# Balancing's product by columns walked row by row, and a new table of turns

## The reference

```
xn = layernorm(x);  s = attention(xn);  g = silu(ffn(xn));  x = x + s * g
```

```
u = -logsumexp(Z + v, over j);  v = -logsumexp(Z + u, over i)     # 50 times
H = exp(Z + u + v);   mixed_i = sum_j H[i, j] * stream_j
```

## Time and profile before

| | |
|---|---|
| median of three runs | 1274.34 us (1271.59 to 1277.91) |
| the profiled execution | 1270.83 us |
| its span, first to last instruction | 1268.8 us |
| TensorE busy (matmul) | 1050.2 us |
| VectorE busy | 834.3 us |
| ScalarE / GpSimd busy | 565.0 / 328.4 us |
| mean granted TensorE clock | 0.908 |

### The profile page before, as it was taken

How to read it: one execution, slowest core, us unless ns; L and a number is a source line. 1 busy time by engine, 2 the same in 40 slices (tenths; PEclk the granted TensorE clock), 3 DMA queues, 4 the chain that set the end, 5 groups by cost and what they waited for, 6 DMA issues and landing times.

```text
span 1268.8 us, 19873 instructions
## 1 busy us (share of the span) xinstructions
PE 1050.2 (83%) x7480; PEld 444.8 (35%) x7480; DVE 834.3 (66%) x1475; ACT 565.0 (45%) x797; POOL 328.4 (26%) x516
## 2 busy tenths in 40 slices
PE   2889999897898997865535639899899988999998
PEld 2434444343333444531211302223233234434344
DVE  6322222001786884798997999888978787876874
ACT  2533333100565664502123335858645767354671
POOL 2145444001776311000002136360000042011230
PEclk9989999998698998786657758999999999999999
DMA  8421220001321011020000032140012111220200
GB/s 306 143 73 55 72 75 25 1 1 49 89 64 35 26 37 60 14 63 22 16 0 1 27 102 74 48 148 28 20 35 69 51 44 39 64 76 26 69 17 34
DMA packets 54899, 69.72 MB, mean 55 GB/s; under 512 B 9526, under 2 KB 43444, under 8 KB 54800
## 3 DMA queue, kind: packets, MB, share of 16 engines
q1 hardware_dynamic: 50828, 58.57, 14.7%
q0 software_dynamic: 3984, 9.98, 2.8%
HBM read 49.45 MB, written 18.82 MB: 54 GB/s over the span
## 4 chain that ended last, share of the span: by engine, by line
DVE 30%; PE 30%; issue 4%; ACT 4%; POOL 3%; DMA 3%; SPq 1%; ACTq 0%; DVEq 0%; POOLq 0%
DVE w_mx L1320 14%; PE w_banks L667 8%; PE w_po L1250 7%; PE w_banks L1230 4%; PE w_banks L1202 3%; DVE w_region L1933 2%; ACT w_pr L1270 2%; PE w_banks L1190 2%; PE w_banks L1584 2%; DVE w_region L1893 1%; DVE w_region L1930 1%; DVE w_region L1928 1%; DVE w_region L1926 1%; DMA w_ks<-stack_scratch 1%; DVE w_region L1924 1%
## 5 line engine op out<-in xcount | busy, mean ns | idle before, releaser
L1320 DVE TENSOR_REDUCE w_mx<-w_banks 128x2 f32<-128x1024 f32 (+3 forms) x352 | 368.6, 1086 | 94.0 <-PE w_banks L1202 92.6
L1270 ACT ACTIVATE w_pr<-w_banks 128x1024 f32<-128x1024 f32 (+1 forms) x312 | 304.2, 1014 | 214.3 <-PE w_banks L1230 201.9
L1308 POOL TENSOR_SCALAR_AFFINE_SELECT w_pr<-w_pr 128x512 f32<-128x512 f32 (+1 forms) x184 | 107.8, 591 | 396.1 <-ACT w_pr L1270 396.1
L1230 PE MATMUL w_banks<-w_qs,w_ks 49*128 49x512 f16 (+7 forms) x832 | 125.4, 346 | 42.9 <-DVE w_mx L1320 30.3
L1202 PE MATMUL w_banks<-w_ks,w_qs 48*128 48x512 f16 (+7 forms) x832 | 139.4, 351 | 25.1 <-DVE w_mx L1320 11.3
L1250 PE MATMUL w_po<-w_pr,w_vz 128*17 128x512 f32 (+7 forms) x1152 | 142.8, 533 | 17.1 <-DVE w_vz L909 6.7
L78 PE MATMUL f_pp<-xt,sl_region 128*128 128x512 f16 x672 | 149.2, 383 | 2.4 <-POOL sl_region L504 2.4
L480 DVE TENSOR_TENSOR sl_region<-sl_region,f_pp 128x512 f32<-128x512 f32 x28 | 19.3, 688 | 120.3 <-ACT sl_region L495 120.3
L78 PEld LDWEIGHTS f_pp<-xt,sl_region 128*128 128x128 f16 x672 | 65.2, 99 | 83.8 <-issue 5.6
L1230 PEld LDWEIGHTS w_banks<-w_qs,w_ks 49*128 49x128 f16 (+1 forms) x832 | 36.0, 97 | 147.1 <-issue 58.3
L1190 PE MATMUL w_banks<-mask_half,ident_half 64*128 64x128 bf16 (+1 forms) x768 | 64.7, 248 | 17.9 <-DMA w_ks<-stack_scratch 8.6
(11 more groups left out here) (221 smaller groups left out, 1478.9 us busy)
## 6 DMA issues: line engine op xcount, KB each, us to landing
stack_scratch<-sl_region SPq DMA_DIRECT2D x102, 128.0 KB
w_qs<-stack_scratch SPq DMA_DIRECT2D x96, 96.0 KB, 2.3
sl_region<-in_L_gu SPq DMA_DIRECT2D x14, 512.0 KB
w_stage<-in_L_w POOLq DMA_DIRECT2D x36, 128.0 KB, 2.4
sl_region<-in_L_down SPq DMA_DIRECT2D x14, 256.0 KB
stack_scratch<-p_qk SPq DMA_DIRECT2D x24, 128.0 KB
w_ks<-stack_scratch SPq DMA_DIRECT2D x32, 96.0 KB, 2.5
...
```

What stands on the lines that cost most here:

```text
L1230: mm = pe.matmul(g.banks.pair_at(f)[:, half, at:at + T - q0], g.ks[base:base + self.rows + 1, k_slot, k_place, j * P:(j + 1) * P], g.qs[ba ...
L1270: act.activation(g.probs.at(self.pr_fill[s])[:, :, 0:width], g.banks.pair_at(self.s_fill[s])[:, :, 0:width], ACT.Exp, scale=self.a.scale). ...
L1308: pool.affine_select(out=diagonal, in_=diagonal, compare_op=ALU.is_ge, fill=0.0, base=0, pattern=pattern, channel_multiplier=-1).then_inc( ...
L1320: dve.tensor_reduce(out, g.banks.pair_at(self.m_fill[m])[:, :, 0:heads * keys].rearrange("q h (p k) -> q h p k", k=keys), AX.X, ALU.max).t ...
```

## The change

Two edits. The product by columns no longer goes column by column through memory (t, j, i) but in memory order (t, i, j); its second operand, the inverse of each column's sum, is then repeated over i, where it was repeated over the innermost index. Each number is multiplied by the same factor as before. And the string `TURNS` is replaced. Every strand keeps its number of ticks.

```diff
         elif step == 5:
-            op = dve.tensor_tensor(bycol, bycol, inverse.rearrange("p (t j) -> p t j", j=n).unsqueeze(3)
+            whole = both.rearrange("p t (i j) -> p t i j", j=n)
+            op = dve.tensor_tensor(whole, whole, inverse.rearrange("p (t j) -> p t j", j=n).unsqueeze(2)
                                    .to_broadcast([P, NT, n, n]), ALU.mult)
...
 TURNS = """
-    w10 m5 q m2 q2 l m t m q m3 e m e t m e m e m2 v e m v e q e v t w2 q e o m2 v m e m v m e2 o m w v e2 w v m w e
...
+    m q4 m7 w10 t m4 e m2 t e m e2 m e v e m2 v q w v w e m w m t e o v m e2 o m2 v e q v e w m w v e2 m v w l o m2
...
-    s18 e s v e b v2 s v e s4 t s4 t s16 o s3 o2 s11 e s3 e2 v e2 v2 e v8 o s v o2 b6 s10 b3 s b6 s b2 s2 b3 s b o
...
+    s17 m s12 m s5 m s3 m s7 o2 s m s5 o s24 q s5 q s17 t o s5 t s7 e2 s9 o s15 w v e2 v e b e o e b v3 e o s e s7
+    v4 o2 b v3 o2 b3 s14 b14 s2 b s2 b s2 b3 s b s b6 s3 b2 s b2 s2 b3 s b8 s b2 s3 b s w s2 w s w s w3 b w6 m w m5
...
```

More of the change, by code:

```diff
@@ L1948 @@
[L1948 to L1962, removed]
@@ L1963 @@
-    r5 v e2 r5 v4 r2 o4 r4 b r5 b2 r3 b17
+    m q4 m7 w10 t m4 e m2 t e m e2 m e v e m2 v q w v w e m w m t e o v m e2 o m2 v e q v e w m w v e2 m v w l o m2
+    t m v q e m o m v e2 v m t q e v q o m2 e v w m e o e w m2 v e2 w2 v m e m t e m w2 o w v m3 v3 e m2 t e m v m e
+    m q o2 q w e w e v m e o e2 v2 e2 t w v m4 v2 m2 w2 o w v w v o2 e m2 t e m o e2 m v m e m v2 e2 v m3 o e o e q
+    v e q m2 v b2 v b m b2 t m t m b m b2 e2 b2 e m b e m b m b11 q v o e2 v e2 v2 t m q m b v e m o2 e m2 b v e m e
@@ new lines @@
+    v3 t e b e b2 m b o2 e m v b4 e v2 e m2 b q o2 m v b e m2 b e2 v q m v s t m2 v2 m2 s b s e o s b o s m s m b m
+    e b s2 e s b2 s b2 s m2 b t m b e2 o v s e v b t e2 s5 e s v o e v b e2 v e2 v2 e v s o2 v s2 m3 v3 o q2 m o q o
+    m b m b5 q b t b m2 b3 w b2 m b2 w b5 q b2 t b5 e b2 e2 m2 b2 e b6 m b m2 s6 m s e s5 m s6 t s8 t s4 b s8 b2 s b
+    s b s3 b2 s b s b s5 b2 s b s b s4 b s14 v2 s v3 s3 o s v s6 q s q s9 e4 b e2 v s b s3 b2 s3 b s4 v2 o s v2 o v
+    o s3 o s3 m s m s2 m s m s2 m s2 m s m s22 m s2 e s12 t e t s4 v2 s5 m s v s v s2 e2 s2 v2 s6 m s4 v s m s5 v
@@ new lines @@
+    s17 m s12 m s5 m s3 m s7 o2 s m s5 o s24 q s5 q s17 t o s5 t s7 e2 s9 o s15 w v e2 v e b e o e b v3 e o s e s7
+    v4 o2 b v3 o2 b3 s14 b14 s2 b s2 b s2 b3 s b s b6 s3 b2 s b2 s2 b3 s b8 s b2 s3 b s w s2 w s w s w3 b w6 m w m5
+    q2 m q2 m2 t m4 e m2 e m2 e m v t m e m e m3 v e b e b w e b3 e2 m v e b5 e b2 q w2 b w t o v b e w3 e w e v e v
+    m e o e m v e b m r m e m v o m e m q v e m2 v e m r t m b r m r q r3 e m2 o v m e m v e o m t m e m q v q b e3
+    b v e2 b3 e m v b2 o e b v o e m2 v e2 o e r m v r m r e b r m3 r b2 m b t r e v m2 b r b2 m2 b2 e m b2 m2 v e
@@ new lines @@
+    b3 o e b m b m t e2 v e m e v e3 q v m e v e m o2 m e2 v t e m2 v e q v m q e m r3 e m v r e2 m r3 m e o2 r m r
+    m v m t e2 o e m v b m r m2 v2 o m e o m b2 t e2 b m b e b2 e2 b4 m b7 v e w e v m w e2 v o v b w5 m2 b e v e r
+    w11 e m e r b m q e r m r t q b m r m r2 o m2 b e v m v m2 v o e w m w e m w t e m o e2 v e3 b v b2 q b e v b2
+    e2 b v m b o e m b m v m e2 v m3 b2 e b3 m2 t b e m v m b e q o q e b m2 v b t o b m b e2 m v m e2 b m e b e m2
+    v b m2 b3 o m e v m w m2 b4 e b v m b e b r e r e r b r3 o b t m b3 m e v e b e o v q r e m e v e m2 v o t m e2
@@ new lines @@
+    v e2 m v m e2 v q2 m w2 e2 w v w2 r o e m3 o e v e v e2 t r m r2 v m v o2 m2 r2 e o m2 r4 m t b2 m e b m b5 t e
+    b2 e b5 e b e b4 v2 e b e b3 o b v2 e2 m v m e m v b o e2 m v q2 m3 r e v o m2 t o b2 q b v m v e m v r m e2 v t
+    r e b e b r m b o b r6 e m o v b r3 e v2 e2 v b m2 b e m e b m3 v o m q2 v m2 b m t b4 m2 b2 m b m b v b2 v b o
+    b o b4 e b t b2 m b2 o m b2 e2 b r t e b e r3 b r e2 v r b4 v e b2 r4 b r e r3 v b2 r2 m v e m q r q r o e m q
+    r2 e v2 m2 v m2 o e2 v m2 o e r m t m v4 m o2 r q e3 r o e r m e r m2 r2 t r2 v m r5 e2 q r m v m r2 b2 v r b m
@@ L1964 @@
+    e v o b3 m b m b e t e b4 m b m b m e b2 m b4 v e2 m t v2 m e o q e m v m2 o e v e2 m v t q m v m2 o q v o e3 v
+    m v2 m o e m2 v o e m r e2 m r2 t m v m v m2 r2 m r2 t m2 r2 e o e r v o v e r e r4 m r2 v r12 e t e2 v2 e v o2
+    e r e2 r2 v3 e v r e r e2 o r5 v o v o v o v r2 o r4 b r2 b r2 b r2 b17
 """
```

## The result

| | before | changed |
|---|---|---|
| median | 1274.34 us (1271.59 to 1277.91) | 1253.13 us (1250.82 to 1254.04) |
| ratio | | 0.9829 [0.9801, 0.9858] |
| the profiled execution / its span | 1270.83 / 1268.8 us | 1254.04 / 1252.1 us |
| TensorE / VectorE busy | 1050.2 / 834.3 us | 1045.7 / 825.3 us |
| ScalarE / GpSimd busy | 565.0 / 328.4 us | 565.3 / 322.3 us |

The medians differ by 21.2 us and the profiled executions by 16.8; a second set of runs gave 1253.14 against 1271.69, 18.6 us. The forecast was 10.

What follows compares the result with a forecast made beforehand. VectorE was taken to bound the kernel around balancing and TensorE the last 200 us. Terms -4.7 - 3.0 - 0.6 - 3.5 + 1.8 = -10.0 us took 1274.34 to 1264 us, range 1253 to 1277.

Steps and rivals of the forecast that it cites:

- The product by columns: In balancing, 50 executions fall from 392 to 297 ns by walking memory in order: -4.7 us, ends 0 and -4.7.
- more than summed: Rival: the first three order terms and the product all reach their best ends, nothing given back: 1257.5 us, chance 0.09.
- VectorE standing before the first mixing step: Sign, behind balancing: if VectorE waits there, the prediction would be wrong as a whole.
- The condition that nothing waits in the stretch: In balancing: the stretch gets about 4.7 us shorter with nothing waiting in it, otherwise the product's term is wrong.
- (a): Near 373 to 393 us: dealing out GpSimd's weight pieces removes TensorE's mask wait and lower clock: -3.0 us, at most 5.3.
- (b): The opening: stacked queries load earlier, ending TensorE's wait at 325.65, against small loads holding SyncE's queue: -0.6 us.
- The rival in which GpSimd falls behind: Scores 18 to 29: added weight pieces delay masks and TensorE waits, so the kernel is slower, 1285 us; chance 0.13.
- (c): Tail of balancing: value products and normalisation issued earlier let TensorE run ahead: -3.5 us, ends -5.6 and +3.3.
- against it: Before mixing: normalisation o43 queues ahead of the first mixing step, so late values cost the same 3.3 us there.
- (d): Behind 744 us: no wait has a clear owner, part of the gain is given back: +1.8 us, bounds -6.5 and +6.5.

Runs made afterwards that it cites:

- e1: The kernel before with only the product edit, keeping the old order table: 1267.98 us, ratio 0.9949.
- e6: The changed kernel with all weight pieces put back about where the old table has them, only GpSimd's order differing: 1270.67 us, ratio 0.9982.
- e7: New product, new order only up to the first normalisation (n10), the old order from there: 1265.3 us, ratio 0.9939.
- e3: New product, new order up to the first balancing tick, the rest in the old order: 1260.66 us, ratio 0.9890.
- e8: The changed kernel with only VectorE's normalisation o41 moved 42 balancing steps earlier, to step 280: 1248.49 us, ratio 0.9811.
- e12: The changed kernel with normalisation o41 at balancing step 280 in place of 322, timed again beside the unaltered changed kernel: 1250.39 us, ratio 0.9834.
- e4: New product, old order up to layer 2's first maxima (m128), the rest in the new order: 1261.37 us, ratio 0.9914.
- e10: New product, new order only from layer 2's first maxima to the start of n31, old order before and after: 1265.91 us, ratio 0.9947.
- e5: Old table with the new product, only the routed layer of half 1 (r24 to r47) placed as in the new table: 1277.02 us, ratio 1.0042.
- e9: New product, old order up to the start of n31, the new order behind it: 1265.56 us, ratio 0.9951.
- e14: The changed kernel with only the routed layer of half 1 (r24 to r47) put back where the old table has it: 1261.06 us, ratio 0.9917.

## Why the prediction was wrong

The sign was right, but the change was 21.2 us where 10 were forecast; the time lies at the very end of the range (1253), and the nearest case was "more than summed" (1257.5), which had been given 0.09. One of the prediction's own signs of being wrong came true, VectorE standing before the first mixing step (2.72 us), though it had meant a slower kernel by it. By its steps:

- **The product by columns: right.** -4.7 forecast, 294 ns measured for 297, -4.9 us of busy time, 5.5 timed alone (e1). The condition that nothing waits in the stretch failed in the changed kernel ("TensorE, half empty there, will not" become late): VectorE stood 2.4 us for scores and 2.1 for ScalarE there, and the stretch shrank by 2.0 us, 129.5 to 127.5. The formula of the Trainium skill ("VectorE: DVE Perf Modes", section on the TRN2 errata) that would have made this term zero prices both products at 291 ns, an estimate; L1931 and L1926 agree with it (294, 292), the old product with 392 does not, so the pattern does count.
- **(a) The block of pieces: right in sign, no term by itself.** The wait of 2.00 us and the lower clock are gone, and n10 begins 3.6 us earlier for (a) and (b) together, as summed; that the sum agrees shows neither part of it. (From 386.26 to 393 it is 6.7 us and not 6.6, so the end of the term is 5.4.) But e6 shows that in the new order the dealing out of the two blocks of pieces is worth some 17.5 us: without it the new order, the product included, is only 2.7 us below the kernel before, less than the product alone. The rival in which GpSimd falls behind was wrong: TensorE's waits for masks before n10 went from 3.7 to 2.9 us.
- **(b) The opening: right**, as far as it can be seen: the wait of 1.23 us at 325.65 is gone. Its size was not measured apart.
- **Not in the sum: 427 to balancing.** The prediction took the entries ahead of balancing as unchanged in count and looked for waits at four places only. TensorE's 4.9 us for stacked keys in this stretch of the trace of before were not among them; 3.9 us between the traces, 4.7 from e7 to e3.
- **(c) The tail: wrong in size.** -3.5 forecast; from the end of balancing to that of the mixing only 0.4 (74.7 to 74.3 us). "TensorE, half idle, can run ahead" failed: the first normalisation (o39) did come 70 steps earlier, the second (o41) stood at s322, and TensorE stood 18.99 us for the bank. The values were then late before the first mixing step, 2.72 us, which is the price that was named "against it". e8 and e12 show that this was the cause of that wait: that one normalisation moved, it goes, and the stretch is 71.2 and 72.0 us. The long mask is gone, as forecast: 6.81 us before, none over 0.77 there now.
- **(d) Everything behind 744: the step that failed.** +1.8 forecast, -6.6 measured (e4), -6.8 between the traces (-16.8 at the end, -10.0 at the last mixing). Two sentences of it were wrong. "No wait there has a clear owner in the new table" was taken as if the old one had none: the trace of before has the same mechanism as (a) a second time, at 1041 to 1044, of 3.00 us, with the lower clock behind it. And "part of what is gained ahead is given back where two nearly full engines meet", in 744 to 880: what was gained went on growing, from 10.0 us at the last mixing step to 11.3 at n30; 1.5 came back between n30 and n31. What the runs show in its place: the new order gets 36 more of TensorE's matmuls done between n30 and n31, and TensorE's idle time from n30 to the end fell from 28.8 to 20.6 us. The cause of that is open. It is not the 3.00 us wait alone: in e10 the wait is gone and the time is that of the product alone, and e5 shortened it and lost 9 us.

Mis-sized together: (d) by 8.6, the unnamed stretch by 3.9 and (c) by 3.1 the other way, with 2.7 of the product hidden between the traces. With the forecast 10.0 that makes, to rounding, the 16.8 us between the profiled executions; the other 4.4 of the 21.2 are the distance of these two executions from their medians. What stays open is what in the order behind layer 1 pays, and whether only unbroken: holes and the clock behind them are there in e5, e9, e10 and e14, but in the changed kernel too, and no run changed the clock alone.
